# Moving the splits of the next layer's weights to other steps of a six-layer local-attention program on one TensorE-bound core

## What is computed

```python
def attn_layer(x, Wqkv, qs, ksc, Wo):
    qkv = x @ Wqkv
    q, k, v = jnp.split(qkv, 3, -1)
    q = l2norm(q) * qs
    k = l2norm(k) * ksc
    q = q * cos * scale + rotate_half(q) * sin * scale
    k = k * cos * inv + rotate_half(k) * sin * inv
    return local_attention(q, k, v).reshape(b, n, INNER) @ Wo

def ffn_layer(x, g, bln, W1, b1, W2, b2):
    xn = (x - mu) / jnp.sqrt(var + 1e-05) * g + bln
    hg = xn @ W1 + b1
    a, gate = jnp.split(hg, 2, -1)
    return a * jax.nn.gelu(gate, approximate=False) @ W2 + b2

for i in range(DEPTH):   # DEPTH = 6
    x = attn_layer(shift_tokens(x), Wqkv[i], q_scale[i], k_scale[i], Wo[i]) + x
    x = ffn_layer(shift_tokens(x), ln_g[i], ln_b[i], W1[i], b1[i], W2[i], b2[i]) + x
```

## Time and profile before

| what | us |
|---|---|
| median of 3 runs | 3686.01 |
| lowest and highest | 3685.73, 3690.58 |
| the profiled execution, whole | 3685.71 |
| its span, first to last instruction | 3683.8 |
| TensorE busy | 3569.0 (97%) |
| ScalarE busy | 3362.8 (91%) |
| VectorE busy | 3130.2 (85%) |
| GpSimd busy | 2745.0 (75%) |

### The profile page before, as it was taken

The page is one execution under the profiler, slowest core; times in us unless marked ns, Lnnn a source line. Parts: engine busy times, 40 slices in busy tenths (PEclk is TensorE's granted clock), DMA queues, the critical chain, the costliest instruction groups (busy, mean ns, idle before and its releaser), DMA issues.

```text
span 3683.8 us, 133067 instructions
## 1 busy us (share of the span) xinstructions
PE 3569.0 (97%) x47348; PEld 3039.1 (82%) x47348; DVE 3130.2 (85%) x7019; ACT 3362.8 (91%) x10923; POOL 2745.0 (75%) x2060
## 2 busy tenths in 40 slices
PE   8999989999999999999999999999999999999998
PEld 5666678888888888888888888888888888888887
DVE  8999888888888788888888888878888888888897
ACT  8999779999999899999999999899998999999996
POOL 0111288888888888788788888888888888888884
PEclk9999999999999999999999999999999999999999
DMA  2000011111111111111111111111111111111111
GB/s 101 7 16 7 10 44 37 36 28 37 42 42 39 32 33 39 38 44 38 33 32 38 40 45 34 32 29 41 49 34 36 30 33 44 33 35 38 41 35 38
DMA packets 165015, 132.71 MB, mean 36 GB/s; under 512 B 113933, under 2 KB 124813, under 8 KB 164109
## 3 DMA queue, kind: packets, MB, share of 16 engines
q1 hardware_dynamic: 164365, 124.19, 13.8%
HBM read 25.84 MB, written 4.19 MB: 8 GB/s over the span
## 4 chain that ended last, share of the span: by engine, by line
PE 75%; DVE 5%; ACT 4%; issue 3%; DVEq 0%; ACTq 0%; POOLq 0%; POOL 0%
PE bank L1067 10%; PE bank L1023 10%; PE bank L1103 8%; PE bank L1048 8%; PE bank L1087 7%; PE bank L985 4%; PE bank L986 4%; PE bank L987 4%; PE bank L946 4%; PE bank L1080 3%; PE bank L919 2%; PE bank L921 2%; ACT a_E L1395 2%; PE bank L920 2%; PE bank L999 2%
## 5 line engine op out<-in xcount | busy, mean ns | idle before, releaser
L1498 POOL TENSOR_TENSOR a_rn<-a_ssqc,a_minus_half 128x16 f32<-128x16 f32 x384 | 1113.3, 2899 | 509.4 <-DVE a_ssqc L1689 499.6
L1395 ACT ACTIVATE a_E<-bank,a_negmax 128x96 f32<-128x96 f32 x3072 | 1012.9, 362 | 23.2 <-DVE a_negmax L1638 22.6
L1519 POOL TENSOR_TENSOR a_r<-a_u,a_rn 128x512 f32<-128x512 f32 x768 | 788.2, 1046 | 0.6
L1506 POOL TENSOR_TENSOR a_PN<-a_E,a_erec 128x384 f32<-128x384 f32 x768 | 739.6, 983 | 11.7 <-PE bank L1048 8.2
L1395 ACT ACTIVATION_READ_ACCUMULATOR a_E<-bank,a_negmax 128x1 f32 x3072 | 707.0, 230 | 0.0
L1378 ACT ACTIVATE a_QK<-bank 128x512 f32<-128x512 f32 x768 | 466.8, 608 | 130.2 <-PE bank L1023 130.1
L1651 DVE TENSOR_TENSOR a_u<-bank,a_rot_c 128x512 f32<-128x512 f32 x768 | 522.0, 680 | 2.4 <-ACT a_sq L1371 2.4
L1661 DVE TENSOR_TENSOR a_v<-bank,a_rot_s 128x512 f32<-128x512 f32 x768 | 522.7, 681 | 0.0
L1371 ACT ACTIVATE a_sq<-bank 128x512 f32<-128x512 f32 x768 | 482.5, 628 | 43.3 <-PE bank L987 13.5
L1023 PE MATMUL bank<-ident,a_r 128*128 128x128 f32 x3072 | 483.4, 280 | 18.3 <-DVE a_bias L1624 11.9
L1356 ACT ACTIVATE a_PT<-bank 128x512 f32<-128x512 f32 x758 | 479.2, 632 | 19.2 <-PE bank L1048 15.2
(11 more groups left out here) (182 smaller groups left out, 8092.6 us busy)
## 6 DMA issues: line engine op xcount, KB each, us to landing
a_V_even<-a_V_odd SPq DMA_DIRECT2D x384, 128.0 KB, 2.3
a_V_even<-a_V_odd SPq DMA_DIRECT2D x192, 64.0 KB, 2.1
a_raw<-in_qkv SPq DMA_DIRECT2D x20, 384.0 KB, 3.6
a_x_sh<-X SPq DMA_DIRECT2D x48, 128.0 KB
a_V_even<-a_V_odd SPq DMA_DIRECT2D x192, 32.0 KB, 2.0
a_x_sh<-X SPq DMA_DIRECT2D x48, 127.0 KB
a_f_sh<-X SPq DMA_DIRECT2D x47, 128.0 KB
a_f_sh<-X SPq DMA_DIRECT2D x47, 127.0 KB
```

Source lines behind the costliest of these rows:

```text
L1395: ins = act.activation(E[:, s.par, k, :], scores[:, i % 2, col:col + KW], ACT.Exp, bias=negmax[:, s.par, k:k + 1], accum_out=esum[:, s.par ...
L1498: pool.tensor_tensor(rn[:, a.par, :], ssqc[:, a.par, :], minus_half[:, :], ALU.pow).then_inc(S["rn"], 1)
L1506: pool.tensor_tensor(PN[:, s.par, 2 * hp:2 * hp + 2, :].rearrange("p i (b k) -> p i b k", b=2)[:, :, :, 0:KW], spread(E[:, s.par, half, :] ...
L1519: pool.tensor_tensor(heads(r[:, a.par, half]), heads(u[:, a.par, half]), rn[:, a.par, mm * 2 * HG:(mm + 1) * 2 * HG].unsqueeze(2).to_broad ...
```

## The change

All computed values stay the same, as do the orders of TensorE, GpSimd and SyncE. Five things move on VectorE and two on ScalarE.

- The low parts of projection weights no longer stand where the high parts do. Groups 0 and 1 go to steps 4 and 5 of the layer's last batch, groups 2 and 3 to steps 2 and 4 of the next layer's first batch. Within the step they stand between the two reciprocals (4), between the first reciprocal and `feed_forward_out` (5), and in front of `turned` (2).
- ScalarE's high part of group 3 goes from step 0 to step 1.
- The low part of the feed-forward matrix goes from step 1 to step 4, between the reciprocals. ScalarE's high part is done in two halves of 341 columns, at the end of steps 0 and 1.
- `biases` goes from behind `norms` to between the first cosines and the first sines.

```diff
+P_SPLIT = ((0, 2), (0, 4), (0, 6), (1, 1))
+P_LOW = ((0, 4), (0, 5), (1, 2), (1, 4))
...
+    def split_at(n, p, places=P_SPLIT):
+        for g, (first, place) in enumerate(places):
+            layer = (n + 1 - first) // NB
+            if (n + 1 - first) % NB == 0 and p == place and 0 < layer < DEPTH:
+                return layer, g
+        return None
...
-                    act.activation(w1h[:, l % 2, :], w.w1[:, :], ACT.Copy, scale=w.cols[:, 0:1]).then_inc(S["w1_hi"], 1)
+                    c = slice(half * DI, half * DI + DI)
+                    act.activation(w1h[:, l % 2, c], w.w1[:, c], ACT.Copy, scale=w.cols[:, 0:1]).then_inc(S["w1_hi"], 1)
...
-                if p == 0:
-                    split_up(n)
-                split_qkv(n, p)
+                if p < 2:
+                    split_up(n, p)
+                split = split_at(n, p)
+                if split:
+                    split_qkv(*split)
...
-                    dve.wait_ge(S["w1_hi"], l + 1)
+                    dve.wait_ge(S["w1_hi"], 2 * l + 2)
...
-                split = split_at(n, p)
+                split = split_at(n, p, P_LOW)
...
                 cosines(n, p, 0)
+                if p == P_BIAS:
+                    biases(n)
                 if p == P_TURN:
+                    split_qkv(n, p)
                     turned(n)
...
                 norms(n, p)
-                if p == P_BIAS:
-                    split_up(n)
-                    biases(n)
                 cosines(n, p, 1)
...
+                if p == P_GATES:
+                    split_qkv(n, p)
+                    split_up(n)
                 if p == P_GELU:
+                    split_qkv(n, p)
                     feed_forward_out(n)
...
-                split_qkv(n, p)
```

More of the change, by code:

```diff
@@ L1335, in gelu, with split_up, split_qkv @@
                     act.activation(gate[:, :, :], gate[:, :, :], ACT.Gelu).then_inc(S["gelu"], 1)
-            def split_up(n):
+            def split_up(n, half):
                 l = prepared(n)
                 if l is not None:
-                    ge(act, S["w1"], 32 * l)
-                    ge(act, S["up"], 2 * NF * NB * (l - 1))
-                    act.activation(w1h[:, l % 2, :], w.w1[:, :], ACT.Copy, scale=w.cols[:, 0:1]).then_inc(S["w1_hi"], 1)
-            def split_qkv(n, p):
-                split = split_at(n, p)
[L1346 to L1350, removed]
+                    if half == 0:
+                        ge(act, S["w1"], 32 * l)
+                        ge(act, S["up"], 2 * NF * NB * (l - 1))
+                    c = slice(half * DI, half * DI + DI)
+                    act.activation(w1h[:, l % 2, c], w.w1[:, c], ACT.Copy, scale=w.cols[:, 0:1]).then_inc(S["w1_hi"], 1)
+            def split_qkv(layer, g):
+                act.wait_ge(S["v"], (layer * NB - 1) * NP + 2 * g + 2)
+                act.wait_ge(S[f"raw{g % 2}"], 16 * (2 * (layer - 1) + g // 2 + 1))
+                high_weights(act, A, raw[:, g % 2, :], g).then_inc(S["w_hi"], 1)
             def probs(t, hp):
@@ L1627, in split_qkv @@
             def split_qkv(n, p):
-                split = split_at(n, p)
+                split = split_at(n, p, P_LOW)
                 if split:
-                    layer, g, count = split
+                    layer, g = split
                     dve.wait_ge(S["w_hi"], G * layer + g + 1)
```

## The result

| kernel | median us | range, runs | before beside it | ratio, 95% interval |
|---|---|---|---|---|
| changed | 3655.83 | 3653.25 to 3657.71, 4 | 3685.99 | 0.9915, 0.9898 to 0.9932 |
| changed, again | 3657.38 | 3654.99 to 3659.34, 5 | 3690.37 | 0.9910, 0.9897 to 0.9924 |
| changed, third time | 3655.86 | 3655.24 to 3657.04, 4 | 3691.29 | 0.9906, 0.9891 to 0.9921 |

The account below looks back on a forecast made before the run. TensorE, busy 97% of the span, was taken as the bound, so only its waits count. Savings 17.1 + 4.5 + 6.9 + 0.5 = 29.0 us from 3685.7 gave 3657 us; range 3649 to 3668.

Parts of the forecast that it names:

- Part 1: Step 1 of five feed-forward-split batches: earlier bias removes TensorE's 2.35 us wait, split free in step 4; 17.1 us saved.
- batch 0: First batch: loses one split where VectorE is never idle, regains it in step 4; 0.5 us saved, between -1 and 1.6.
- Part 2: Layer's last batch, groups 0 and 1 moved to steps 4 and 5: wait before `down` goes; 5 x 0.89 = 4.5 us.
- Part 3: Group 2's low part leaves step 6, before the next batch's input: 0.87 us saved per boundary, some 0.1 wait left.
- Part 4: Group 3's low part leaves step 0 for step 4 of the same first batch: 1.3 us saved per boundary.
- Part 5: Step 2 of a layer's first batch: group 2's low part before a_f_xl takes 1.58 us, costing 0.8 per boundary.
- rival 2: Low parts in steps 4 and 5 wait for GpSimd's power; about 1.5 us per boundary, 3665 us; chance 0.04.
- Rival 1: TensorE's clock still falls: three to six moments at 1.2 GHz, 1.7 us each, 3662 to 3667 us; chance 0.14.
- Rival 3: Better: group 2's low part meets the power or a GpSimd gap, rotation tables hide too; 3652 us; chance 0.10.
- Rival 4: Another condition holds the transposes, and ScalarE holds TensorE at boundaries; only some 5 us go, 3679 to 3686; chance 0.07.
- Rival 5: Slower: group 2's low part before a_f_xl holds TensorE, needing 7.3 us per boundary beyond the 0.8; chance 0.03.

Follow-up runs that it names:

- the three variants of step 2: Changed kernel with ScalarE's group 3 high part moved to step 2 (3655.83 us), group 2's splits moved to steps 5 and 6 (3656.16), or both (3655.26).
- the boundaries alone: Changed kernel with biases and both feed-forward matrix splits put back as before, so only the projection weights' splits moved: 3675.00 us, ratio 0.9969.

## Why the prediction was right, and where it wasn't

The places and the mechanisms came out as forecast. The total is closer than its terms, and that part is luck: Part 1 gave 0.8 us less than forecast, the boundaries 1.4 more, batch 0 1.0 more, the ordinary batches took 2.0 and the later start and the last batches 0.7 that had no term, so that 29.0 became 27.9.

**Part 1** was forecast at 17.1 and gave 16.3. The mechanism held at each point: no wait, clock 1.00, 66.54 to 66.65 for a batch with the bias alone moved, and 8.24 - 7.05 = 1.19 us in step 1 for the one-column matmuls. The missing 0.8 is 0.15 a batch, 66.69 instead of 66.54. The second half of ScalarE's a_w1h costs 0.12 in step 2, where 0.05 was priced, since `turn` waits 0.2 us for the a_QK behind it; the other 0.08 is about what every ordinary batch lost too, for which see below. That the split is free in step 4 held; it took 0.90 us there. But so it would have been in step 1: with the bias first, nobody waited for the split in its old place.

**Part 2** was forecast at 4.5 with 0.89 per boundary; step 5 fell from 10.76 to 9.89, 0.87. **Part 3** said 0.87 in the next step 7 with 0.1 left: 9.32 fell to 8.45, 0.87. What is left is 0.4, not 0.1, since I took a small wait of 0.1 for the whole cost of the rotation tables, while VectorE has no idle time in this step. **Part 4** said 1.3; step 1 gave 1.22.

**Part 5** is the term that was mis-sized: 0.8 was taken off for step 2 in each boundary, and the step took 0.43 more than before. That it is 0.81 above an ordinary step 2 now is not the forecast come true, because it was 0.38 above it before the change already, which the prediction left out. And the low part takes 1.39, not 1.58: I took the length from another place with the same neighbour on GpSimd, but it depends on how much of that neighbour's work is left (see rival 2). The input's low part began 1522.02 - 1515.45 = 6.57 us into the step before and 1510.79 - 1503.65 = 7.14 now, 0.57 later where 0.9 was expected, and 0.43 of it shows in the step. So the five boundaries gave 12.8 us in place of 4.5 + 6.9 = 11.4. The sentence that VectorE's own lateness covers ScalarE's held as well, with a margin of 0.3 us that only the experiments could measure.

**Batch 0** was given 0.5. The profiled executions say 1.5, but the changed kernel's second profile has 48.01 there, at a mean granted clock of 0.93, against 48.10 before: 0.1. The difference goes with the clock at the start, where the same stretch has a mean of 0.90 before (48.10) and 0.95 in the changed kernel (46.63). Of the six profiles whose batch 0 is in the changed order (the changed kernel's three and the three variants of step 2), five have 46.6 and one 48.0; in the kernel before and the three with only a part of the change it is 47.9 to 48.1. Whether the change makes the better start more likely or it is chance, no run here shows.

```profile
467.07:515.17 48.10, 39.63 (x376) 31.86 (x377) 44.18 (x66) 31.86 (x98) 39.11 (x27) 0.90 0.15 33
```

```profile
467.69:514.32 46.63, 37.21 (x376) 29.99 (x377) 42.70 (x66) 32.31 (x99) 39.17 (x27) 0.95 0.15 34
```

**The ordinary batches** had no term, and cost 0.07 each, 2.0 in all: the one loss nobody forecast. It is in every kernel in which either half of Part 1 was made (1953.7 to 1954.6 for the thirty), and in neither of those without it (1952.1 and 1952.2 with the boundaries alone). The page's group of exponentials, before and with the bias alone moved, moves with it (with the boundaries alone changed it is 1013.1, 362):

```profile
L1395 ACT ACTIVATE a_E<-bank,a_negmax 128x96 f32<-128x96 f32 x3072 | 1012.9, 362 | 23.2 <-DVE a_negmax L1638 22.6
```

```profile
L1395 ACT ACTIVATE a_E<-bank,a_negmax 128x96 f32<-128x96 f32 x3072 | 1015.9, 364 | 22.9 <-DVE a_negmax L1638 22.3
```

ScalarE is busy over nine tenths of the time, and it does the same instructions there. I can say where the time goes, not why; this stays open.

**Rival 1**, a clock that still falls, did not happen: 1.00 in all fifteen stretches of the three kinds, also where TensorE now waits 0.47 us in step 2. **Rival 2**, low parts that wait for the power, is refuted by this profile: all fifteen low parts in steps 4 and 5 began about 0.52 us after a power, ended under it and took 0.92 to 0.93 us, and the power took no longer than its 2.90. The prediction's own evidence for this was thinner than it reads. Of the ten low parts of 0.95 before, the five in step 2 had 0.81 us of a power beside them, but the five in step 6 only its last 0.33; for the rest of these the product that GpSimd began beside them took 1.34 us, where two such products of the earlier trace rows take 1.61 together. The long low parts follow a rule of their own. Each ended 0.92 us after a point that lies 0.10 to 0.11 us before the end of the product that GpSimd was in as the low part began: 1509.94 against 1510.05 and 1476.97 against 1477.08 in the rows above. The 1.58 of the earlier trace rows at 1474.59 fits too, beside a product that ended at 1475.35. In all the kernels run, each low part of 1.30 to 1.58 us keeps this distance, 0.10 to 0.11. I read it so: VectorE stood until the product was over and then ran at full speed, and GpSimd's next product stood for it, which is the 2.76 us. The Trainium skill (SBUF — State Buffer, Who interferes with whom) says that a VectorE instruction with two SBUF inputs contends with GpSimd's reads, and calls the shared ports an exclusive lock; that whoever issues first keeps them for a whole instruction it says of VectorE's two-port modes, which the prediction carried over to this subtraction. The trace bears out both for the products on 128x384 and 128x512. For the power on 128x16 it decides against them, in all fifteen cases. **Rival 3** was right in its direction, since step 2 cost 0.43 instead of 0.8, but by neither of its means: the low part met a product and not the power or a gap, and the rotation tables don't hide. **Rival 4** had the waits' names against it, and the names were true, except that ScalarE does hold `turn` in step 2 now. **Rival 5** lay in the right place, step 2, with 0.43 us per boundary where it needed 8.

## What to carry to other kernels

Where one engine is busy 97% of the span, the excess lengths over an ordinary repetition are about all that moving work of the other engines can give back, and the waits by name say to whom each part is owed. Sized so, the three places that lost a low part came out within 0.1 us each. The one that gained a low part was off by 0.37, because neither the length of the low part there nor the step's own excess before the change had been read from that place: measure the receiving place too. When an instruction goes into a wait, ask which other engine is late at the same place and by how much less, for that is what the next move will find. And of two things that stand between a producer and a waiting engine, move the small one that is waited for ahead, before moving the large one away: the bias ahead gave all of it, the split away little more than half.

## What I had not expected of the hardware

- The clock falls behind a wait of 2.35 to 2.5 us in three of five batches, in the same program and execution, and not in the same three in another kernel. It never fell behind 1.52 us (0 of 5). A fall costs 1.6 to 1.8 us (70.50 to 70.73 against 68.94). What decides between equal waits isn't explained by any run here.
- A low part on VectorE that begins while GpSimd is in a product takes 0.92 us plus what is left of the product less 0.1: 1.30, 1.39 and 1.58 at different places. GpSimd's power, longer than any of them with 2.90 us, holds it up not at all. That it reads only 16 elements of a partition may be the reason, but no run varied its size.
- Batch 0 took 46.6, 47.9 to 48.1 or 48.8 us in the profiled executions, and the part from batch 47 on 125.8 to 126.0 or 127.2 to 127.8, the changed kernel having both of 46.6 and 48.0, and both of 126.0 and 127.7. Some 1.5 us at either end can differ between executions of one kernel, which is a reason why moves worth 2 us can be read from the stretches and not from the medians.
